# Nine phases on one core: parts on four row groups, attention in units of eight heads, last two stages rewritten

## The reference

```python
# level 0, first layer: 16 experts, one chosen by each sequence
h = gelu(einsum('bnd,hd->bnh', x, fc1_w) + fc1_b, approximate=False)     # hidden 512
shared = einsum('bnh,sh->bns', h, fc2_w) + fc2_b                         # 96 columns
expert_x = einsum('bnh,bph->bnp', h, experts_w[indices]) + experts_b[indices][:, None, :]   # 32 columns
# level 2, six layers: 16 heads of 64, local attention with a window
q, k, v = split(shift_tokens(x) @ Wqkv, 3)
q = l2norm(q) * qs; k = l2norm(k) * ks                                   # then rotary tables
sim = where(mask, -max, einsum('bhwie,bhwje->bhwij', q, k) * 8)
x = einsum('bhwij,bhwje->bhwie', softmax(sim), v) @ Wo + x
# level 3, first layer: 16 heads of 8, keys of the token before plus the query's own key
weights = softmax(concat([where(mask, q k_prev * SCALE, -inf), (q * k_self).sum() * SCALE]))
attn = weights[:-1] @ v_prev + weights[-1:] * v_self; y = attn @ Wo + bo
# level 3, feed-forward: activations, hidden and weights quantised in blocks of 16 (FP4 with FP8 scales)
hidden = silu(nvfp4(y, s_in) @ nvfp4(gate_w)) * (nvfp4(y, s_in) @ nvfp4(up_w))
out = x + nvfp4(hidden, s_in_down) @ nvfp4(down_w)
```

## Time and profile before

| | us |
|---|---|
| three runs, median | 9264.65 (9260.26 to 9271.44) |
| profiled execution, span | 9259.6 |
| PE busy | 7948.2, 86% |
| DVE busy | 4604.8, 50% |
| ACT busy | 3202.1, 35% |
| POOL busy | 3263.2, 35% |

### The profile page before, as it was taken

The page is one execution under the profiler, slowest core; times in us unless marked ns, Lnnn a source line. Parts: engine busy times, 40 slices in busy tenths (PEclk is TensorE's granted clock), DMA queues, the critical chain, the costliest instruction groups (busy, mean ns, idle before and its releaser), DMA issues. The chain is left out here.

```text
span 9259.6 us, 150161 instructions
## 1 busy us (share of the span) xinstructions
PE 7948.2 (86%) x43190; PEld 5640.0 (61%) x43190; DVE 4604.8 (50%) x10196; ACT 3202.1 (35%) x7426; POOL 3263.2 (35%) x2508
## 2 busy tenths in 40 slices
PE   1999689999489789999989989999998998999922
PEld 0444366666234378768858857876885884777710
DVE  1111200000533178768858858866885884333378
ACT  0000000000311056546646646655664663222211
POOL 1000100000100078658838838855874882000000
PEclk9999899999588599999989999999999998555555
DMA  5222222222000000000000000000000000000000
GB/s 118 52 51 52 51 52 50 50 50 50 3 20 3 5 13 0 10 3 0 0 12 0 0 12 0 0 10 3 0 0 12 0 0 3 3 2 2 2 7 6
DMA packets 442422, 163.38 MB, mean 18 GB/s; under 512 B 405846, under 2 KB 432535, under 8 KB 435391
## 3 DMA queue, kind: packets, MB, share of 16 engines
q1 hardware_dynamic: 288721, 124.55, 6.1%
q10 hardware_dynamic: 153600, 37.77, 1.8%
HBM read 100.58 MB, written 61.67 MB: 18 GB/s over the span
## 5 line engine op out<-in xcount | busy, mean ns | idle before, releaser
L1345 POOL TENSOR_TENSOR rs<-ss,minus_half 128x8 f32<-128x8 f32 x768 | 1264.8, 1647 | 798.1 <-DVE ss L1407 796.3
L393 PE MATMUL o_ps<-o_w,z_fm 128*128 128x256 bf16 (+1 forms) x8192 | 1092.2, 279 | 148.9 <-DMA o_w<-rows_exs 112.4
L393 PEld LDWEIGHTS o_ps<-o_w,z_fm 128*128 128x128 bf16 x8192 | 783.5, 96 | 457.9 <-DMA o_w<-rows_exs 116.7
L268 PE MATMUL h_ps<-h_x,h_w 128*128 128x512 bf16 x4096 | 886.0, 380 | 194.2 <-DMA h_x<-rows_xs 194.2
L1348 POOL TENSOR_TENSOR t<-t 128x512 f32<-128x512 f32 x768 | 976.0, 1271 | 0.0
L1165 PE MATMUL qk_ps<-wqkv,xs 128*128 128x512 f32 x1536 | 814.3, 612 | 101.7 <-DVE xs L1382 80.9
L1352 POOL TENSOR_TENSOR qk<-t,rs 128x512 f32<-128x512 f32 x768 | 800.9, 1043 | 76.0 <-POOL t L1348 31.4
L268 PEld LDWEIGHTS h_ps<-h_x,h_w 128*128 (+1 forms) x4096 | 401.1, 98 | 678.5 <-DMA h_x<-rows_xs 194.2
L1397 DVE TENSOR_TENSOR t<-qk_ps,rot 128x512 f32<-128x512 f32 x768 | 531.9, 693 | 526.9 <-ACT sq L1276 526.9
L1183 PE MATMUL s_ps<-kT,qT 128*128 128x256 f32 x3072 | 791.2, 380 | 0.0
L1200 PE MATMUL att_o_ps<-v,pT 128*128 128x65 f32 x6144 | 771.2, 268 | 0.0
(11 more groups left out here) (317 smaller groups left out, 12567.2 us busy)
## 6 DMA issues: line engine op xcount, KB each, us to landing
rows_hs<-h_parts ACTq DMA_DIRECT2D x384, 96.0 KB, 1.9
z_fm<-rows_hs SPq DMA_DIRECT2D x256, 144.0 KB
o_w<-rows_exs SPq DMA_DIRECT2D x256, 72.0 KB
rows_xs<-s_xp SPq DMA_DIRECT2D x24, 384.0 KB, 4.5
rows_exs<-s_exp SPq DMA_DIRECT2D x36, 256.0 KB, 4.8
h_x<-rows_xs SPq DMA_DIRECT2D x128, 72.0 KB
wqkv<-in_wqkv SPq DMA_DIRECT2D x6, 1536.0 KB, 6.5
wo<-in_wo SPq DMA_DIRECT2D x6, 512.0 KB, 6.9
```

The lines of the kernel that those rows point to most:

```text
L268: mm = pe.matmul(banks[t][:, :], w1[:, bass.ds(i * 2 * KC + (c * KC + k - e * P // 2), 1), t, :] .rearrange("p a n -> p (a n)"), x[:, 2 * ...
L393: mm = pe.matmul(bank[:, 0:2 * P], hc[:, cc, t, :], w[:, bass.ds(i * 2 * TC + (cc * TC + t), 1), :].rearrange("p a n -> p (a n)"), start=f ...
L1345: pool.tensor_tensor(rs[:, i, :], ss[:, i, :], R.minus_half[:, 0:2 * UH], ALU.pow).then_inc(s_["rs"], 1)
```

## The change

Level 0: `split` takes the high halves of the f32 words by a strided read instead of a cast; the stored weights lie as the host laid them out, so that 18 stores with long pieces take the place of 48; there are no memsets. In hidden and out the nine rows stand four times in the tiles, at rows 0, 32, 64 and 96: in hidden for the four hidden tiles t of one feature, in out for four sequences b. Each of the four matmuls has its own bank. To fill them, every chunk of x is loaded four times, and out loads hs and exs for each sequence into its rows. In out even and odd features add up in two halves of a bank, with N = 128.

Attention: a unit is eight heads (64 a layer). Scores are eight matmuls with 64 rows, in pairs on rows 0 and 64, into two banks; ACT exponentiates in place in PSUM with the row minimum as bias and sums the denominators; DVE normalises p before its transposes; values gives the transposed output in two column groups, so that `turn_o` is gone; `project` adds to the residual in every unit. There is one qk_ps and one s_ps (of two banks), and squares waits for both rotations.

level3_cond: all 16 heads of one sequence in a unit, four row groups for masks and scores, four column groups for values and denominators, projections for four sequences at once. level3_ffn: two sequences a unit (four for tokens), four large operations of hidden's chain on POOL, copies on ACT, one pass for the three weights. The core of the diff:

```diff
-    t(0, eng.tensor_copy(parts(2), src))
+
+    def high(a):
+        v = a.bitcast(BF16)
+        return bass.AP(v.tensor, v.offset + 1, [v.ap[0]] + [[2 * s, n] for s, n in a.ap[1:]])
+    t(0, eng.tensor_copy(parts(2), high(src)))
     t(1, eng.tensor_tensor(rest, src, parts(2), ALU.subtract))
-    t(2, eng.tensor_copy(parts(1), rest))
+    t(2, eng.tensor_copy(parts(1), high(rest)))
...
-                pool.memset(shp[:, :, :, :, :], 0.0).then_inc(zero, 1)
-                pool.memset(exp_[:, :, :, :, :, :], 0.0).then_inc(zero, 1)
...
+                for r in range(ROWS):
+                    sp.dma_start(T["w2s"][r].rearrange("b (c t) o -> (b c) (t o)", c=32), shp[:, r % PARTS, :]
+                                 ).then_inc(out, 16)
...
+                def load(g, i, c):
+
+                    sp.wait_ge(used, at(g * NC + i * 4 + c - 4))
+                    for t in range(HT):
+                        sp.dma_start(x[rows(t), c, :, :].rearrange("p k n -> p (k n)"),
+                                     T["xs"][bass.ds(g, 1), :, bass.ds(i * 4 * KC + c * KC, KC), :]
+                                     .rearrange("a p k n -> (a p) (k n)")).then_inc(loaded[c], 16)
...
+                    for i in range(NC):
+                        pe.wait_ge(loaded[i % 4], dma_at((k * (NC // 4) + i // 4) * 4 + 3))
+                        for f in range(KC):
                             for t in range(HT):
-                                mm = pe.matmul(banks[t][:, :],
-                                               w1[:, bass.ds(i * 2 * KC + (c * KC + k - e * P // 2), 1), t, :]
-                                               .rearrange("p a n -> p (a n)"),
-                                               x[:, 2 * e + c, k, :], start=first, stop=False, skip_group_check=True)
+                                mm = pe.matmul(ps[c][t][:, :], w1[rows(t), i * KC + f, :], x[rows(t), i % 4, f, :],
+                                               start=i + f == 0, stop=False, skip_group_check=True)
                         mm.then_inc(used, 1)
-
...
-                        act.activation(low[:, t, :], low[:, t, :], ACT.Gelu, bias=0.0).then_inc(act_, 1)
+                        act.activation(h[:, t, :], ps[c][t][:, :], ACT.Gelu, bias=fc1b[:, t:t + 1]).then_inc(act_, 1)
...
-                            sp.dma_start(hc[rows, cc, :, :].rearrange("p t n -> p (t n)"),
-                                         T["hs"][bass.ds(j, 1), :, s, :].rearrange("a p t n -> (a p) (t n)")
-                                         ).then_inc(loaded[cc], 16)
-                            sp.dma_start(w[rows, s, 2 * SHARED:2 * P],
-                                         T["exs"][bass.ds(r, 1), :, s, :].rearrange("a p t n -> (a p) t n")
-                                         ).then_inc(loaded[cc], 16)
+                            for b in range(GB):
+                                sp.dma_start(hc[rows(b), cc, :, :].rearrange("p t n -> p (t n)"),
+                                             T["hs"][bass.ds(j * GB + b, 1), :, s, :]
+                                             .rearrange("a p t n -> (a p) (t n)")).then_inc(loaded[cc], 16)
+                                sp.dma_start(w[rows(b), 3, s, :].rearrange("p t o -> p (t o)"),
+                                             T["exs"][:, bass.ds(r[b], 1), s, :]
+                                             .rearrange("p a t o -> (p a) (t o)")).then_inc(loaded[cc], 16)
...
+                        for t in range(TC):
+                            for b in range(GB):
+                                mm = pe.matmul(ps[c][b][:, (t % 2) * P:(t % 2) * P + P], hc[rows(b), i % 2, t, :],
+                                               w[rows(b), :, i * TC + t, :], start=i + t == 0, stop=False,
+                                               skip_group_check=True)
+                        mm.then_inc(used, 1)
...
-                    for n in range(2):
-                        mm = pe.matmul(s_ps[:, c % 2, n * 2 * P:(n + 1) * 2 * P], qT[:, c % 2, n, :],
-                                       kT[:, c % 2, n, :, :].rearrange("p e k -> p (e k)"),
-                                       start=False, stop=True, skip_group_check=True)
+                    pe.wait_ge(s_["kTc"], at(k))
+                    pe.wait_ge(s_["p0"], at(k - 1))
+                    pe.wait_ge(s_["p1"], at(k - 1))
+                    for e in range(2):
+                        pe.matmul(s_ps[:, e, :], R.identb[:, :], mask[:, :, :].rearrange("p h k -> p (h k)"),
+                                  start=True, stop=False, skip_group_check=True)
+                    for i in range(4):
+                        for e in range(2):
+                            r = slice(DH * e, DH * e + DH)
+                            mm = pe.matmul(s_ps[:, e, i * P:(i + 1) * P], qT[r, c % 2, i, :], kT[r, c % 2, i, :],
+                                           start=False, stop=True, skip_group_check=True)
                     mm.then_inc(s_["scores"], 1)
...
-                    for h in range(UH):
-                        mm = pe.matmul(oh_ps[:, h, :], pT[:, c % 2, h, :], v1[:, c % 8, h, :],
-                                       start=True, stop=True)
+                    for i in range(4):
+                        for e in range(2):
+                            d = (2 * i + e) * DH
+                            mm = pe.matmul(oT_ps[DH * e:DH * e + DH, i * P:(i + 1) * P], v[:, c % 8, d:d + DH],
+                                           pT[:, c % 2, e, i, :], start=True, stop=True, skip_group_check=True)
...
-                    pipeline(pe, NU, 8, [(project, 8), (turn_o, 7), (values, 6), (turn_p, 5), (scores, 3), (turn_qk, 2),
-                                         (qkv, 0)], k0=l * NU)
+                    pipeline(pe, NU, 8, [(turn_q, 2), (project_q, 0), (turn_p1, 4), (turn_k, 2), (project_k, 0),
+                                         (values, 4), (turn_p0, 3), (project_v, 0), (scores, 2), (project, 4)],
+                             k0=l * NU)
...
                 def squares(k, j, c):
-                    act.wait_ge(s_["qkv"], at(k))
+                    act.wait_ge(s_["t2"], at(k))
...
+                def exps(k, c, e):
+                    act.wait_ge(s_[f"low{e}"], at(k))
+                    for i in range(4):
+                        ins = act.activation(s_ps[:, e, i * P:(i + 1) * P], s_ps[:, e, i * P:(i + 1) * P], ACT.Exp,
+                                             bias=low[:, c % 2, e, i:i + 1], scale=-1.0,
+                                             accum_out=den[:, c % 2, e, i:i + 1])
...
-                    pipeline(act, NU, 8, [(keep_o, 7), (keep_p, 5), (exps, 4), (keep_qk, 2), (squares, 0)], k0=l * NU)
+                    pipeline(act, NU, 8, [(keep_q, 2), (keep_p1, 4), (exps1, 3), (keep_k, 2), (keep_o, 4), (keep_p0, 3),
+                                          (keep_v, 0), (squares, 0), (exps0, 2)], k0=l * NU)
...
-                    pipeline(dve, NU, 8, [(shift, 0), (residual, 8), (normalise, 6), (softmax, 3), (sums, 0)],
-                             k0=l * NU)
+                    pipeline(dve, NU, 8, [(normalise0, 4), (shift, 0), (rotate, 1), (normalise1, 4), (rotate_swapped, 1), (lows, 3),
+                                          (sums, 1), (residual, 5)], k0=l * NU)
...
+                    for g in (2 * half, 2 * half + 1):
+                        r = slice(32 * g, 32 * g + 1)
+                        pe.matmul(s_ps[:, g, :, :], onesb[r, :],
+                                  mrow[r, c % 2, :].unsqueeze(1).to_broadcast([1, 4, S]),
+                                  start=True, stop=False, skip_group_check=True)
+                    for g in (2 * half, 2 * half + 1):
+                        r = slice(32 * g, 32 * g + 32)
+                        mm = pe.matmul(s_ps[:, g, :, :].rearrange("p h k -> p (h k)"), qT[r, i, seq(c)],
+                                       k4[r, i, c % GS, :, :].rearrange("p h k -> p (h k)"),
+                                       start=False, stop=True, skip_group_check=True)
...
+                        for g in range(4):
+                            v = (4 * g + h) * 32
+                            pe.matmul(o_ps[32 * g:32 * g + 32, 0, :], vz[:, c % 2, v:v + 32],
+                                      pT[:, g, h * S:(h + 1) * S], start=h == 0, stop=h == 3, skip_group_check=True)
...
+                        for g in range(4):
+                            mm = pe.matmul(o_ps[32 * g:32 * g + 32, 1, :], onez[:, h * 32:h * 32 + 32],
+                                           pT[:, g, h * S:(h + 1) * S], start=False, stop=h == 3,
+                                           skip_group_check=True)
...
+                pipeline(pe, B, 2 * GS, [(first, 5), (turn_low, 6), (second, 5), (turn_high, 6),
+                                         (project, 1), (output, 7), (values, 6)])
...
+                    pool.wait_ge(s_["vb"], at(k - 2))
```

(8 more changed lines are left out.)

1280 lines of the change are left out of this document (681 added, 599 removed).

## The result

The changed kernel takes 7,267.76 us (median of four runs, 7,264.73 to 7,271.26) against 9,263.61 us of the kernel before (four runs, 9,260.26 to 9,271.44): ratio 0.7845, 95% interval 0.7834 to 0.7856. The forecast was 7,750 with a range of 7,350 to 8,350: the sign was right, the gain of 1,996 us lies 82 us outside the range. The profiled execution has a span of 7,269.4 us.

A forecast was written before the change was run, and what follows sets the result against it. The prediction took PE to bound hidden and lead in the attention, and DVE to bound level3_ffn. 9,260 - 89 (start) - 409 (hidden) + 12 (gap) - 292 (out) - 180 (attention) - 407 (level3_cond) - 148 (level3_ffn) gave 7,750, range 7,350 to 8,350.

The forecast's parts named there:

- No engine alone sets the unit; a loop does: Attention: the loop over the single qk_ps, 7.1 us plus five hand-overs of 0.2, sets the eight-head unit.
- the 8.1 of the loop: Attention: one round through qk_ps, from project_q to the next, takes 8.1 us with its hand-overs.
- I take 9.0: Attention: a unit takes 9.0 us, so a layer 611 us against 641, and six layers -180.
- The forecast's lower end: Attention: the favourable end, 8.3 us a unit, for -450 us over six layers.
- I take 6.5: Out: a chunk takes 6.5 us from issue, load and PE, plus 25 for the groups: 860 us, -292.
- The rival that bytes bind level 0: Hidden and out: nine-row loads give only 60 GB/s, hidden 770, out 920, total about 8,100; chance 0.13.
- PE 1.7: Hidden: PE needs 1.7 us a chunk with four matmuls side by side, less than the loads.
- the sign that was named for being right: Hidden: matmuls about 110 ns apart on average, with PE waiting for x.
- At 1.2 GHz a f32 matmul costs 0.52: level3_cond: price of a matmul with N=128, behind 16.5 us a sequence, 555 us in all, -407.
- the rival on the clock: Attention: the clock falls to 1.2 GHz, about 16 us a unit, +450 a layer, total 10,400; chance 0.03.
- The attention's loop is not longer than PE: Denies the rival that the attention's loop is longer than the engines: 10.9 us a unit, total 8,480; chance 0.10.
- row and column groups do run side by side: Denies the rival that they do not: hidden stays 889, out 1,270, level3_cond 1,020, total 9,760; chance 0.04.

The follow-up runs named there:

- att_extra_visit: The changed kernel with one full-array bf16 matmul of 128 columns added in the middle of the attention's scores: 7,398.88 us.
- out_ring4: The changed kernel with out's hs loads on ACT's queue, exs in four larger pieces a group, and four hs slots of 16 steps instead of two of 32: 7,114.43 us.
- hid4_k32: The changed kernel with hidden's four row groups each read with 32 rows, the nine and 23 of zeros: 7,319.07 us.
- hid1_half: The changed kernel with hidden on one row group alone and half of its matmuls left out: 7,691.64 us.
- cond_finish: The changed kernel with masks and finish moved ahead of attend_high in DVE's list of level3_cond: 7,165.20 us.
- hid4_warm: The changed kernel with 32 matmuls on all 128 rows added before the first chunk of hidden and again before out: 7,279.81 us.

## Why the prediction was wrong, point by point

**Attention, the term that broke the range** (-180 taken, -478 measured). The failed step is "No engine alone sets the unit; a loop does", and with it "I take 9.0". PE's own sum there was right: 7.4 in pairs, and up to 0.8 for the changes, 8.2; the trace has 8.33. But the forecast added the 0.8, which is PE's, to the 8.1 of the loop, which is not. It should have taken the larger of 8.2 and 8.1. The loop had room as well, as the same unit shows on DVE and ACT:

```profile
3206.24 1.23 DVE L1391 TENSOR_TENSOR t<-qk_ps,rot 128x1024 f32<-128x1024 f32 x1 [0.60 <-PE qk_ps L1129]
...
3208.19 1.21 DVE L1397 TENSOR_TENSOR t<-qk_ps,rot 128x1024 f32<-128x1024 f32 x1
...
3209.44 1.02 ACT L1255 ACTIVATE sq<-qk_ps 128x1024 f32<-128x1024 f32 x1
```

From project_q (3203.22) to the end of the squares (3210.46) are 7.24 us, and PE starts the next project_q only at 3211.56, 1.1 us later. The hand-overs that can be read here are small: project_k ends at 3206.20 and the first rotation starts at 3206.24, the second ends at 3209.40 and the squares start at 3209.44, 0.04 us each where the forecast took 0.2. The size of a change of division was sound: 0.2 forecast, 0.15 read from att_extra_visit. (The Trainium skill, "TensorEngine Tiling (Array Packing)", Key Properties, says that such a change drains TensorE; the runs agree in that it costs time.) 64 units at 8.33 are 533 us, and fill and drain 24 where 35 were taken: from its first to its last projection the attention takes 557.5 us in a layer, against 642 before and the 611 forecast. Of these 85 us a layer some 5 are lost again in the unchanged rest of the layer, which leaves six times 80. The forecast's lower end, 8.3 a unit, was the right value.

**Out** (-292 taken, -379 measured). The failed step is "I take 6.5": two chunks take 12, not 13. Its model, load time plus issue plus PE in a ring of two, was the right mechanism, as out_ring4 showed, but two of its pieces were off and partly cancelled. PE's chunk was put at 1.8 to 2.4 and is 3.60, since it runs at 1.2 GHz; issue and load, put at 8.4 to 12, are 7.2 to 7.5 together, so the loads of a chunk overlap its issues. The other 25 us for the groups were too many as well: 128 x 6.0 = 768 leaves 12 of the 780. The rival that bytes bind level 0 was wrong: with more slots the same loads moved 78 GB/s instead of 64. In hidden the traffic was 161 GB/s, of which the loads of x, 37.7 MB in 442 us, are 85 and the rest stores; in hid4_k32 chunks of 288 KB followed each other at 2.46 us around 160 us, 120 GB/s of nine-row loads. So four loads to four groups of rows don't share the 60 GB/s that the load of w1 had.

**Hidden** (-397 with the gap, -434 measured). Here the number was close by accident. "PE 1.7" a chunk failed: it is 32 x 107 = 3.42, which happens to be the 3.4 that was taken for the loads. So the sign that was named for being right, a mean distance of about 110 ns, came true for another reason than the one given, and its other half, PE waiting for x, did not: PE is idle for 4.4 of the 442 us. Where PE did run at 2.4 GHz for most of the time (hid4_k32, mean clock 0.90), hidden took 427 us from its first matmul to its last instead of 441, with PE busy for 254 of them and waiting for x; a chunk then takes 427 / 128 = 3.3 us. So the price of the loads was about right, and the higher clock was worth only 14 us there. Whether a load's issues, its latency or its bytes set these 3.3 us is not shown.
The Trainium skill, "TensorE: Matmul & The Clock Gate", Part 1, says that sustained matmul activity releases the throttle. Here 437.83 us of matmuls in 442.20 did not, and 5 us of them undid it; the measurement decides. The Trainium skill, same page, Part 3, has four row groups gain 3.07 times at K = 32 and N = 512; with nine rows, in hid1_half one matmul takes 427 ns and in the changed kernel four do, a factor of 4.0.

**level3_cond** (-407 taken, -481 measured). The failed step is "At 1.2 GHz a f32 matmul costs 0.52", in two ways. The granted clock is 0.79, not the 0.50 of the earlier trace rows. And 0.52 is too dear even at 1.2 GHz: it divides a duration, 2.07 us, in which the last matmul's end is counted; the instructions of the earlier trace rows start 213 ns apart, two to a matmul, so 0.43. PE is busy for only 303 of 400 us, and a sequence takes 13.3 us at the median instead of 16.5. What held the phase was in part the circle of PE and DVE that cond_finish opened. 14 of the 74 us that the forecast missed come from the base (962 for 976). That values run side by side was right: undone, they cost 67 us.

**Start, gap, level3_ffn.** -92 for -89; the gap is 100.5 for 100; level3_ffn is -127 for -148, by its own window 300.5 us from the first matmul, where 300 was forecast: the miss of 21 lies in the time before, taken from a window of 448 that began earlier than the phase's first matmul.

**Slips in the working.** None of them moved the forecast. POOL's 7.4 should be 7.8 by its own terms (2.7 + 2 x 2.54); the trace has 2.91 + 1.90 + 2.36 = 7.2. In the rival on the clock 64 x 16 + 35 is 418 a layer above 641, not 450; the 10,400 is right with 418.

**Rivals.** The clock was at its lower level, but in hidden and out, not in the attention, where it is 0.97. The earlier trace rows had a hint that the forecast named and did not use for level 0: level3_cond at 0.50 with PE busy for 90% of the window, some of it on 32-row tiles. The attention's loop is not longer than PE, and row and column groups do run side by side. The misses, 298 + 87 + 74 + 37 + 3 - 21, make 478 of the 482 us between 7,750 and 7,268; the rest is rounding. All but one have one sign, and the range had been built as if the stages erred by themselves: with the attention's miss of 298 alone the time would have lain inside it.

## What to carry to other kernels

When a stage has both an engine's sum and a loop's, take the larger; a cost that belongs to one is not added to the other. A matmul's rate is read from the distance of its starts, column count over time, and not from a printed clock: tiles with few rows, even four side by side, can leave TensorE at 1.2 GHz with the engine 99% busy. Before loads are called bound by their bytes, one kernel with more and smaller slots of the same buffer shows whether they are; here it was worth 153 us, and the issues, twice as many, are then the next thing to look at. And where an engine waits for another in turn, the order of the stages in its list is worth a try: two stages moved in level3_cond gave 100 us, half of it through the clock.

## What the runs showed that I had not expected

- Four groups of 32 rows, 23 of them zeros, raised the clock to 2.4 GHz; four of 16, two of 32, and four, two or one of nine did not. A clock raised by full matmuls was lost after 5 us of nine-row tiles without a gap between them (hid4_warm).
- In hid4_k32 the clock rose, but PE then waited for loads, and it fell again and again; in out it was 0.50 throughout. That kernel was slower in total, by 51 us, of which 14 are memsets before the first matmul and 30 a longer way from the first matmul of hidden to out.
- A full-array matmul put among 64-row ones cost 0.3 us at 2.4 GHz beside its own 0.05 (att_extra_visit).
- A second queue took 2% off out; four slots of half the size, with the second queue and larger pieces of exs, took 21% off it.
